# Attention in a perceiver block: scores in three fp32r terms, three keys blocks at the head of a phase, and GpSimd's split in quarters

## The chip, the cores and the metric

The kernel runs on one core of a Trainium2 chip. The metric is the time of one execution on the device in microseconds (us). Engines: TensorE (PE, its weight loads PEld), VectorE (DVE), ScalarE (ACT), GpSimd (POOL), and SyncE (SP), whose queue issues the DMAs. Results of PE go to PSUM, which has eight banks; a bank holds 128 x 512 float32 values.

## The reference

```python
x = x + xattn(layernorm(x), ctx, ctx)   # 16 heads of 32: x (2,128,512), ctx (2,2048,512)
x = x + attn(layernorm(x))              # 16 heads, reshaped without a transposition, layernorm with gamma, beta
x = x + ffn(layernorm(x))               # the expert of 4 that the router's argmax names, gelu, Wo, layernorm
# xattn, for each of 16 heads:
q = Q @ Wq + bq;  k = K @ Wk + bk;  v = V @ Wv + bv
out = softmax(q @ k.T / sqrt(32)) @ v   # then out @ Wo + bo
```

All data are float32. The context (2 x 2048 rows) makes the first attention the largest part of the work.

## The kernel before, in words

The first attention is cut into eight **phases** p = 0 to 7 (NP = 8, G = 4): batch b = p // 4, and in it a group g of four heads (128 of the 512 columns). A phase goes over four blocks c of 512 keys (C = 4, CH = 512). Every engine's program is written out by hand in its order, with waits on semaphores; there is no planner.

**Keys** (`keys`, PE from line 972, DVE line 586). A block's keys, transposed, are the product of the group's columns of Wk with the context, 4 tiles of 128 x 3 terms = 12 products of 512 columns in fp32r: weights and context are each split into a high part in fp32r and the rest (wkH, wkL, ctxH, ctxL), and three of the four cross terms are taken. All products of this form go through the helper `product`, line 969. They land in one bank (K_BANK, 6), and DVE adds the bias and writes `Kr` (line 592). The next keys block waits on PE until DVE has read the bank (`k_done`, line 980).

**Scores** (`scores`, line 1003): four heads, each a float32 product of 32 rows with 512 columns, in banks 0 to 3 (line 1018). DVE's `negative_scores` (line 603) reads each bank, negates, keeps the running minimum and writes `Pm`; the next block's scores of a head wait for that (`s_done`).

**Softmax.** When a phase's four blocks are scored, ACT's `exponentials` (line 367) take a head's 2048 scores at a time. In the *next* phase, PE transposes the probabilities, four 128 x 128 tiles per head and block (`probs_T`, line 1021, operation in line 1032), heads 0 and 2 into bank 4, heads 1 and 3 into bank 5 (T_BANKS). ACT copies heads 0 to 2 to `PT` (line 378), DVE head 3 (line 621). `weighted_values` (line 1036, operation in line 1047) multiplies with V in bank 7.

**The end of a phase.** DVE's `reciprocals` (line 624) inverts the sums and spreads them over 128 columns (`rexp`, line 631); PE's `reciprocals_T` (line 1052) puts them across partitions; ACT copies that to `RT` (line 386); DVE's `outputs` (line 634) multiplies and adds the bias. The first weighted values of a phase wait for the outputs of the phase before (`o_done`).

The main loop of PE (from line 1275) does, in iteration p, the keys and scores of phase p and the transposes and weighted values of phase p - 1:

```python
if more: keys(p, 0)
if late: weighted_values(p - 2, C - 1); reciprocals_T(p - 2)
if more: keys(p, 1)
for c in range(C):
    probs_T(p - 1, c, 0); probs_T(p - 1, c, 1)
    if c == 0 and more: keys(p, 2)
    if c: weighted_values(p - 1, c - 1)
    probs_T(p - 1, c, 2); probs_T(p - 1, c, 3)
    if more:
        scores(p, c)
        if c == 1: keys(p, 3)
```

`late` is true from p = 2 on, except in p = 5. At p = 4 (= G) the loop also does the first batch's second attention and the second batch's 16 value blocks (`while_values`) between each other. Batch 0's later steps are spread over phases 5 to 7 as DVE's `alongside` (line 821): in phase 5 the reciprocals of the second attention's sums (`denominators2`, line 728), its normalised output (`outputs2`) and that output's transposition (`outputs2_T`, line 739, 16 copies); in phase 6 PE's `attention2_out` (line 1175), which writes bank 0 and whose result DVE reads in `added_output2` (line 754) before the scores of phase 6 may write that bank (`u_done`); in phase 7 the router's logits in bank 1, which DVE reads (line 771) before the scores of phase 7 (`logit_done`).

**The context of batch 1** is loaded when phase 3's keys have read batch 0's, and POOL splits it, per block one cast of 128 x 2048 (line 339) and one subtraction (line 341). Phase 4's keys wait for the subtraction (`ctx_split1`).

**SP** loads the second attention's weights one after the other into one tile, `wS` (lines 256 to 262): xWo early, then wq, wk, wv, wo when the last user is done. After the phases come second_experts, first_experts (line 1217) and the output product (line 1271), which the change does not touch.

Of the kernel before, what the change touches and what calls it, by code (L numbers as in the profile page):

```python
# [11 lines left out]
F32 = mybir.dt.float32  # L12
# [5 lines left out]
P = 128  # L18
# [5 lines left out]
def perceiver_block(nc, a, out):  # L24
# [23 lines left out]
    with ExitStack() as ctx:  # L48
# [25 lines left out]
        Kr = at("Kr", [P, C, CH], F32, 176)  # L74
        x = at("x_sb", [P, B, D], F32, 192)
        qT = at("qT", [P, G, TOK], F32, 196)
        attnT = at("attnT", [P, G, TOK], F32, 200)
# [9 lines left out]
        wS = at("wS", [P, KT, D], F32, 184)  # L87
        xbo = at("xbo", [P, D], F32, 184)
# [78 lines left out]
        K_BANK, PV_BANK = 6, 7  # L167
        SPARE = K_BANK
# [35 lines left out]
        k_mm, k_done = sem("k_mm"), sem("k_done")  # L204
# [29 lines left out]
        def _(sp):  # L234
# [21 lines left out]
            sp.wait_ge(x_added, B)  # L256
# [3 lines left out]
            for k, w in enumerate(("wk", "wv", "wo")):  # L260
                sp.wait_ge(qkv_mm[0], k + 1)
                sp.dma_start(wS[:], a[w]).then_inc(wS_in, 16)
            sp.wait_ge(v_mm, B * NV)
            for n in range(3):
# [46 lines left out]
        def _(pool):  # L311
# [24 lines left out]
            for c in range(C):  # L336

                pool.wait_ge(raw_in[c], 32 if c else 16)
                pool.tensor_copy(ctxH[c][:], raw[c][:]).then_inc(ctx_hi1, 1)
                pool.wait_ge(ctx_hi1, c + 1)  # L340
                pool.tensor_tensor(ctxL[c][:], raw[c][:], ctxH[c][:].bitcast(F32), ALU.subtract).then_inc(ctx_split1, 1)
# [6 lines left out]
        def _(act):  # L348
# [32 lines left out]
            def reciprocals_T(p):  # L381

                act.wait_ge(r_mm, p + 1)
                if p:
                    act.wait_ge(o_done, 2 * p)
                act.copy(RT[:], ps[:, PV_BANK, P:2 * P]).then_inc(r_copied, 1)

# [11 lines left out]
            for c in range(1, C):  # L399
                for j in (0, 2):  # L400
                    values(0, c, j)
# [39 lines left out]

            def masks(b):
# [20 lines left out]
            for p in range(1, NP + 1):  # L463
                late = p >= 2 and p != G + 1
                if p != G + 1:
                    exponentials(p - 1, 0)
                    exponentials(p - 1, 1)
                    if late:
                        reciprocals_T(p - 2)
                    exponentials(p - 1, 2)  # L470
                probs_T(p - 1, 0, 0)
# [963 lines left out]
```

## Time and profile before

| | us |
|---|---|
| median of 3 runs | 538.05 |
| their lowest and highest | 537.7, 540.35 |
| the profiled execution's own time | 536.02 |
| its span, from the first to the last instruction | 534.3 |
| busy: PE, PEld, DVE, ACT, POOL | 516.1, 367.6, 294.6, 210.0, 38.3 |
| mean granted clock of TensorE | 0.998 of full speed |

The page has for each engine its busy time and share, the chain of work that ended last, and groups of instructions with the mean duration of one and the idle time ahead of them. Records of PE overlap, because a product's end lies behind the start of the next: the pace is the distance between starts, not the duration. The columns of the trace's other views stand with the rows below.

### The profile page before, as it was taken

Reading aid. Unit: us, or ns where it says so; the run is one execution under the profiler, and the core shown is the slowest. Engines: PE = TensorE matmul, PEld = TensorE weight load, DVE = VectorE, ACT = ScalarE, POOL = GpSimd, SP = SyncE. Lnnn points to the kernel's source line nnn. Section 1 sums busy time; section 2 is a strip of 40 time slices with the busy share of each in tenths; the row PEclk is TensorE's granted clock in tenths of the full one; section 3 lists DMA queues with packets and bytes.
Section 4 is the critical chain, followed back from the end, with each engine's and each line's share of the span. In section 5 each row is a group of like instructions: output and inputs, shape, how many; then the busy total and the mean of one; then the engine's idle time right before and its main releaser. Section 6 shows DMA issues by size and latency. Waiting matters only on the chain.

```text
span 534.3 us, 8854 instructions
## 1 busy us (share of the span) xinstructions
PE 516.1 (97%) x3574; PEld 367.6 (69%) x3574; DVE 294.6 (55%) x606; ACT 210.0 (39%) x305; POOL 38.3 (7%) x32
## 2 busy tenths in 40 slices
PE   8999999999998999999999999988999999999995
PEld 6777776677776777888776678746575445877652
DVE  3645525757576662453496684652275537976332
ACT  4110027273736331455126346373065206745120
POOL 0220000000395000000000000000000010000000
PEclk9999999999999999999999999999999999999999
DMA  8800000000450002330100000590986965874000
GB/s 260 351 0 1 1 0 1 2 1 3 168 216 11 2 2 79 106 132 0 60 2 1 1 2 1 224 404 10 360 340 230 389 253 216 305 284 197 1 20 20
DMA packets 11598, 62.21 MB, mean 116 GB/s; under 512 B 1572, under 2 KB 2596, under 8 KB 4772
## 3 DMA queue, kind: packets, MB, share of 16 engines
q1 hardware_dynamic: 11560, 61.66, 30.7%
q8 instruction: 29, 0.48, 0.4%
q14 instruction: 9, 0.07, 0.0%
HBM read 61.13 MB, written 0.52 MB: 115 GB/s over the span
## 4 chain that ended last, share of the span: by engine, by line
PE 95%; DVE 2%; issue 2%; ACT 1%; POOLq 0%; POOL 0%; DVEq 0%; ACTq 0%
PE ps L969 41%; PE ps L1032 11%; PE ps L1224 10%; PE ps L1018 6%; PE ps L1047 6%; PE ps L1271 5%; PE ps L1251 3%; PE ps L1252 3%; PE ps L1253 3%; PE ps L963 1%; PE ps L1060 1%; PE ps L1234 1%; PE ps L1148 1%; PE ps L1065 1%; PE ps L1069 1%
## 5 line engine op out<-in xcount | busy, mean ns | idle before, releaser
L378 ACT COPY PT<-ps 128x512 f32<-128x512 f32 x96 | 53.3, 588 | 105.1 <-PE ps L1032 105.1
L1032 PEld LDWEIGHTS ps<-ident,Pm 128*128 128x128 f32 x512 | 56.5, 141 | 21.7 <-issue 18.1
L1032 PE MATMUL ps<-ident,Pm 128*128 128x128 f32 x512 | 69.2, 277 | 1.6 <-ACT PT L378 0.7
L612 DVE TENSOR_SCALAR_CACHE_REDUCE Pm<-ps,small 128x512 f32<-128x512 f32 x96 | 66.4, 748 | 7.1 <-PE ps L1018 6.9
L370 ACT ACTIVATE Pm<-Pm,small 128x2048 f32<-128x2048 f32 x32 | 64.2, 2009 | 14.2 <-DVE Pm L612 14.2
L1224 PE MATMUL ps<-w1raw,z 128*128 128x512 f32 x128 | 57.3, 595 | 0.7 <-DVE Pm L612 0.7
L969 PE MATMUL ps<-ctxH,wkH 128*128 128x512 f32 x124 | 51.4, 414 | 2.4 <-DVE Kr L592 2.1
L969 PE MATMUL ps<-wvH,ctxH 128*128 128x512 f32 x124 | 50.0, 403 | 0.0
L969 PE MATMUL ps<-ctxL,wkH 128*128 128x512 f32 x124 | 48.7, 393 | 0.0
L969 PE MATMUL ps<-ctxH,wkL 128*128 128x512 f32 x124 | 48.5, 391 | 0.0
L969 PE MATMUL ps<-wvH,ctxL 128*128 128x512 f32 x124 | 48.4, 390 | 0.0
L969 PE MATMUL ps<-wvL,ctxH 128*128 128x512 f32 x124 | 48.3, 389 | 0.0
L592 DVE TENSOR_SCALAR Kr<-ps,small 128x512 f32<-128x512 f32 x32 | 24.0, 749 | 36.4 <-PE ps L969 34.4
L1224 PEld LDWEIGHTS ps<-w1raw,z 128*128 128x128 f32 x128 | 23.5, 190 | 27.1 <-issue 26.4
L943 DVE TENSOR_TENSOR w2L<-w2raw,w2H 128x2048 fp32r<-128x2048 f32 x16 | 36.2, 2288 | 10.1 <-ACT w2H L547 10.1
L621 DVE COPY PT<-ps 128x512 f32<-128x512 f32 x32 | 22.1, 691 | 30.3 <-PE ps L1032 29.4
L969 PEld LDWEIGHTS ps<-ctxH,wkH 128*128 128x128 f32 x124 | 23.3, 188 | 20.5 <-issue 15.8
L1018 PE MATMUL ps<-Kr,qT 32*128 32x512 f32 x256 | 36.5, 640 | 0.6 <-ACT qT L397 0.6
L547 ACT CAST w2H<-w2raw 128x2048 fp32r<-128x2048 f32 x16 | 30.4, 1910 | 15.1 <-PE ps L1253 15.0
L365 ACT COPY V<-ps 128x512 f32<-128x512 f32 x16 | 9.4, 588 | 66.3 <-PE ps L969 64.4
L1047 PE MATMUL ps<-PT,V 128*32 128x128 f32 x1024 | 34.6, 276 | 0.9 <-DVE PT L621 0.9
L324 POOL TENSOR_TENSOR small<-small 128x1 f32<-128x1 f32 x10 | 6.8, 678 | 372.1 <-DVE small L572 372.1
(162 smaller groups left out, 720.3 us busy)
## 6 DMA issues: line engine op xcount, KB each, us to landing
w1raw<-in_W SPq DMA_DIRECT2D x16, 1024.0 KB, 7.2
w2raw<-in_W SPq DMA_DIRECT2D x16, 1024.0 KB, 4.8
raw<-in_ctxT SPq DMA_DIRECT2D x7, 1024.0 KB, 4.8
woF<-in_ffn_Wo SPq DMA_DIRECT2D x4, 1024.0 KB, 15.9
ctx_first<-in_ctxT SPq DMA_DIRECT2D x4, 256.0 KB, 5.0
wv_raw<-in_xWv SPq DMA_DIRECT2D x2, 512.0 KB, 6.6
wq<-in_xWq SPq DMA_DIRECT2D x1, 1024.0 KB, 11.7
wS<-in_xWo SPq DMA_DIRECT2D x1, 1024.0 KB, 7.0
```

What stands on the lines that cost most here:

```text
L370: act.activation(Pm[:, i, :], Pm[:, i, :], ACT.Exp, bias=mx[:, p % 2, i, C - 1:C], scale=-1.0, accum_out=den[:, p, i:i + 1]).then_inc(exp_ ...
L378: act.copy(PT[:, c % 2, i, :, :].rearrange("p k t -> p (k t)"), ps[:, T_BANKS[i % 2], :]).then_inc(pt_act, 1)
L547: act.copy(w2H[n % 3][:], w2raw[n % RING2][:]).then_inc(w1_hi, 1)
L592: dve.tensor_scalar(Kr[:, c, :], ps[:, K_BANK, :], bias3[:, 1, p % G:p % G + 1], None, ALU.add).then_inc(k_done, 1)
L612: dve.tensor_scalar(Pm[:, i, c * CH:(c + 1) * CH], ps[:, i, :], -1.0, mx[:, p % 2, i, c - 1:c] if c else NOT_YET, ALU.mult, ALU.min, accum ...
L943: dve.tensor_tensor(w2L[n % RING2][:], w2raw[n % RING2][:], w2H[n % 3][:].bitcast(F32), ALU.subtract).then_inc(w1_split, 1)
L969: mm = pe.matmul(dst, l, r, start=(n == 0), stop=(n == len(pairs) - 1))
L1018: pe.matmul(ps[:, i, :], qT[q, g, b * T:(b + 1) * T], Kr[q, c, :], start=True, stop=True)\
L1032: last = pe.transpose(ps[:, T_BANKS[i % 2], j * P:(j + 1) * P], Pm[:, i, c * CH + j * P:c * CH + (j + 1) * P], ident[:])
L1047: last = pe.matmul(ps[q, PV_BANK, 0:T], V[:, c * JT + j, (HPG * g + i) * DH:(HPG * g + i + 1) * DH], PT[:, c % 2, i, j, :], start=(c == 0 ...
L1224: last = pe.matmul(ps[:, c, :], z[:, n, :], w1raw[n % RING][:, c * CH:(c + 1) * CH], start=(n == 0), stop=False)
L1271: last = pe.matmul(ps[:, b, :], hidT[b][:, k, :], woF[:, k, :], start=(k == 0), stop=(k == IT - 1))
```

## The change

Scores are computed in fp32r, in three terms as the keys are: ACT writes the keys with their bias as a high part (`KrH`), DVE the rest (`KrL`), each for three blocks (KR = 3) instead of four; the queries are split likewise at the start (`qH` by ACT, `qL` by DVE). A scores block is 12 products instead of 4. In phases 1 to 7 three keys blocks stand in a row at the head, into banks 6, 3 and 2 (`K_BANKS`), where banks 3 and 2 are those of the scores of heads 3 and 2. The weighted values and reciprocals of p - 2 follow them. The copies of a phase's first transposes (block 0, four heads) are all DVE's, those of blocks 1 to 3 all ACT's. The copy to `RT` moves from ACT to DVE. POOL splits a block in quarters: four casts, four subtractions. `wS` moves to another place and is loaded later, and the second attention's output weight has tiles of its own (`wo2`), loaded once per batch; half of `outputs2_T(0)` goes to ACT; in the part with the value blocks some of these move by one place.

```diff
+        K_BANKS = (K_BANK, 3, 2, K_BANK)
...
-            sp.wait_ge(x_added, B)
+            sp.wait_ge(pv_mm, C * G)
             sp.dma_start(wS[:], a["xWo"]).then_inc(wS_in, 16)
...
+                if n == 7:
+                    sp.wait_ge(qkv_mm[1], 2)
+                    sp.dma_start(wo2[1][:], a["wo"]).then_inc(wo2_in[1], 16)
...
+                for k in range(KT):
+                    pool.tensor_copy(ctxH[c][:, k, :], raw[c][:, k, :]).then_inc(ctx_hi1, 1)
+                for k in range(KT):
+                    pool.wait_ge(ctx_hi1, KT * c + k + 1)
+                    pool.tensor_tensor(ctxL[c][:, k, :], raw[c][:, k, :], ctxH[c][:, k, :].bitcast(F32), ALU.subtract)\
+                        .then_inc(ctx_split1, 1)
...
+            def keys(p, c):
+
+                n = p * C + c
+                bank = K_BANKS[c] if p else K_BANK
+                act.wait_ge(k_mm, n + 1)
+                if n >= KR:
+                    act.wait_ge(s_mm, (n if c == C - 1 else p * C) * HPG - (2 * HPG if c == C - 1 else 0))
+                act.activation(KrH[:, c % KR, :], ps[:, bank, :], ACT.Identity, bias=bias3[:, 1, p % G:p % G + 1],
+                               scale=1.0).then_inc(k_hi, 1)
...
+                act.activation(qH[:, m, :], ps[:, (m + 2) % 4, 0:TOK], ACT.Identity, bias=bqs[:, m:m + 1],
+                               scale=SCALE).then_inc(q_done, 1)
...
+                for c in range(C - 1):
+                    if p != G + 1:
+                        exponentials(p - 1, c)
+                    if p < NP:
+                        keys(p, c)
...
+                dve.wait_ge(k_hi, n + 1)
+                dve.scalar_tensor_tensor(KrL[:, c % KR, :], ps[:, bank, :], bias3[:, 1, p % G:p % G + 1],
+                                         KrH[:, c % KR, :].bitcast(F32), ALU.add, ALU.subtract).then_inc(k_done, 1)
...
+                dve.wait_ge(r_mm, p + 1)
+                dve.tensor_copy(RT[:], ps[:, PV_BANK, P:2 * P]).then_inc(r_copied, 1)
...
-                if p == G + 2 and at_point == "keys1":
+                if p == G + 2 and at_point == "outputs":
                     added_output2(0)
...
                     keys(p, 0)
                     alongside(p, "keys0")
                     keys(p, 1)
+                    alongside(p, "keys1")
+                    keys(p, 2)
+                for i in range(HPG):
+                    probs_T(p - 1, i)
                 if late:
                     outputs(p - 2)
-                alongside(p, "keys1")
-                if p < NP:
-                    keys(p, 2)
+                alongside(p, "outputs")
                 for c in range(C):
-                    probs_T(p - 1, c)
                     if p < NP:
                         negative_scores(p, c)
...
+                if p == G + 1 and c == 2:
+                    pe.wait_ge(rden_ready, 1)
...
+                if p and 0 < c < C - 1:
+                    pe.wait_ge(s_done, p * C * HPG)
...
+                terms = ((qH, KrH), (qL, KrH), (qH, KrL))
+                for k, (l, r) in enumerate(terms):
+                    for i in range(HPG):
+                        q = slice(DH * i, DH * (i + 1))
+                        if n and k == 0:
+                            pe.wait_ge(s_done, (n - 1) * HPG + i + 1)
+                        last = pe.matmul(ps[:, i, :], l[q, g, b * T:(b + 1) * T], r[q, c % KR, :], start=(k == 0),
+                                         stop=(k == len(terms) - 1))
...
                 if more:
                     keys(p, 1)
+                    keys(p, 2)
+                if late:
+                    weighted_values(p - 2, C - 1)
+                    reciprocals_T(p - 2)
...
-                    if c == 0 and more:
-                        keys(p, 2)
```

## Rows read from the trace of the kernel before

**Rows 1.** The page: busy time of each engine, and the chain's shares by line.

```profile
PE 516.1 (97%) x3574; PEld 367.6 (69%) x3574; DVE 294.6 (55%) x606; ACT 210.0 (39%) x305; POOL 38.3 (7%) x32
...
PE ps L969 41%; PE ps L1032 11%; PE ps L1224 10%; PE ps L1018 6%; PE ps L1047 6%; PE ps L1271 5%; PE ps L1251 3%; PE ps L1252 3%; PE ps L1253 3%; PE ps L963 1%; PE ps L1060 1%; PE ps L1234 1%; PE ps L1148 1%; PE ps L1065 1%; PE ps L1069 1%
```

**Rows 2.** Table by stage: phases 2 and 4, length, then each engine's busy time.

```profile
105.71:133.92 28.21, 28.15 (x278) 20.51 (x275) 17.34 (x44) 14.86 (x21) 0.00 (x0) 1.00 0.01 2
162.15:192.82 30.67, 28.46 (x278) 20.58 (x275) 20.25 (x46) 14.98 (x21) 5.70 (x2) 1.00 0.00 1
```

**Rows 3.** Waits of PE: what it waited for, total us, times, longest.

```profile
PE ps L969 <- DVE Kr L592: 2.1, 3, 0.9
PE ps L1055 <- DVE rexp L631: 1.9, 1, 1.9
```

**Rows 4.** Timeline of PE, phase 2's head and phase 3's start: start, duration.

```profile
105.71 0.50 PE L969 MATMUL ps<-ctxH,wkH 128*128 128x512 f32 x1
106.05 0.39 PE L969 MATMUL ps<-ctxH,wkL 128*128 128x512 f32 x1
...
109.92 0.47 PE L969 MATMUL ps<-ctxH,wkH 128*128 128x512 f32 x1
...
116.69 1.03 PE L1032 MATMUL ps<-ident,Pm 128*128 128x128 f32 x8
117.65 1.14 PE L1018 MATMUL ps<-Kr,qT 32*128 32x512 f32 x8
118.73 1.09 PE L1032 MATMUL ps<-ident,Pm 128*128 128x128 f32 x8
...
133.92 0.50 PE L969 MATMUL ps<-ctxH,wkH 128*128 128x512 f32 x1
```

**Rows 5.** Chain in order of time: start, length of the piece, its records.

```profile
46.97 1.07 PE ps L1018 x8
48.04 13.82 PE ps L969 x60
...
395.23 3.44 PE ps L1224 x8
```

**Rows 6.** Timeline of all engines: one scores block, its loads and its products.

```profile
104.64 0.31 PEld L1018 LDWEIGHTS ps<-Kr,qT 32*128 32x128 f32 x8 [0.17 <-issue]
104.64 1.14 PE L1018 MATMUL ps<-Kr,qT 32*128 32x512 f32 x8
```

**Rows 7.** Timelines of POOL and of DVE, head of phase 4.

```profile
163.34 4.59 POOL L341 TENSOR_TENSOR ctxL<-raw,ctxH 128x2048 fp32r<-128x2048 f32 x1
...
165.14 2.87 DVE L631 COPY rexp<-small 128x128 f32<-128x128 f32 x1
```

**Rows 8.** Timeline of DVE: last negative scores of phase 2, first of phase 4.

```profile
136.03 0.75 DVE L612 TENSOR_SCALAR_CACHE_REDUCE Pm<-ps,small 128x512 f32<-128x512 f32 x1
...
177.71 0.69 DVE L612 TENSOR_SCALAR_CACHE_REDUCE Pm<-ps 128x512 f32<-128x512 f32 x1 [0.36 <-PE ps L1018]
...
178.33 0.69 DVE L612 TENSOR_SCALAR_CACHE_REDUCE Pm<-ps 128x512 f32<-128x512 f32 x1
```

**Rows 9.** Timeline, phase 8: a copy on DVE and PE after it.

```profile
359.88 0.69 DVE L621 COPY PT<-ps 128x512 f32<-128x512 f32 x1 [5.05 <-PE ps L1032]
...
360.72 0.63 PE L1032 MATMUL ps<-ident,Pm 128*128 128x128 f32 x4 [0.34 <-DVE PT L621]
```

**Rows 10.** Groups by line: count, busy us, mean ns of one, idle before.

```profile
L378 ACT COPY PT<-ps 128x512 f32<-128x512 f32 x96 | 53.3, 588 | 105.1 <-PE ps L1032 105.1
L621 DVE COPY PT<-ps 128x512 f32<-128x512 f32 x32 | 22.1, 691 | 30.3 <-PE ps L1032 29.4
L731 DVE RECIPROCAL qT<-ps 128x512 f32<-128x512 f32 x1 | 3.3, 3346 | 0.0
L640 DVE TENSOR_TENSOR attnT<-ps,RT 128x128 f32<-128x128 f32 x8 | 2.3, 284 | 5.4 <-ACT RT L386 5.4
L397 ACT ACTIVATE qT<-ps,small 128x256 f32<-128x256 f32 x4 | 1.9, 473 | 5.8 <-PE ps L969 5.8
```

More of the change, by code:

```diff
@@ L379, in probs_T @@
                          ps[:, T_BANKS[i % 2], :]).then_inc(pt_act, 1)
[L381 to L386, printed above, removed]
+            act.wait_ge(bias_in, 16)
+            keys(0, 0)
             for j in (0, 2):
@@ L440, in values2, with outputs2_T @@
                 act.copy(V2[b][:].rearrange("p g d -> p (g d)"), ps[:, 4 * b, :]).then_inc(v2_ready, 1)
+            def outputs2_T(b):
+                act.wait_ge(cN_ready, b + 1)
+                for i in range(2, HPG):
+                    for a in range(HPG):
+                        act.copy(cT[b][DH * a:DH * (a + 1), :, :]
+                                 .rearrange("p m (g i t) -> p m g i t", i=HPG, t=TPH)[:, :, :, i, :],
+                                 cN[b][DH * i:DH * (i + 1), :, :].rearrange("p g (t c) -> p g t c", t=TPH)[:, :, :, a::HPG]
+                                 .rearrange("p g t m -> p m g t")).then_inc(cT_act[b], 1)
             def masks(b):
@@ L668, in _ @@
             values(0, 0, 3)
+            for m in range(G):
+                dve.wait_ge(q_done, 2 * (m + 1))
+                dve.tensor_tensor(qL[:, m, :], qT[:, m, :], qH[:, m, :].bitcast(F32), ALU.subtract).then_inc(q_split, 1)
             negative_scores(0, 0)
@@ L675, in _ @@
                     values(0, c, j)
+                if c == 1:
+                    dve.wait_ge(xbo_in, 16)
+                    dve.wait_ge(norm_done, B)
+                    for b in range(B):
+                        dve.tensor_tensor(x[:, b, :], x[:, b, :], xbo[:], ALU.add).then_inc(x_added, 1)
+                    dve.wait_ge(x_added, B)
                 negative_scores(0, c)
@@ L851, in alongside @@
                     dve.tensor_copy(yT[0][:], split4(ps[:, XT_BANKS[0], :])).then_inc(x2T_done, 1)
-                if p == G + 3 and at_point == "keys1":
+                if p == G + 3 and at_point == "outputs":
                     logits(0)
@@ L983, in keys @@
                 f = slice(g * P, (g + 1) * P)
-                product(ps[:, K_BANK, :], [(w[:, k, f], t[:, k, :]) for k in range(KT)
+                if p and 0 < c < C - 1:
+                    pe.wait_ge(s_done, p * C * HPG)
+                product(ps[:, K_BANKS[c] if p else K_BANK, :], [(w[:, k, f], t[:, k, :]) for k in range(KT)
                                            for w, t in ((wkH, ctxH[c]), (wkL, ctxH[c]), (wkH, ctxL[c]))]).then_inc(k_mm, 1)
@@ L1013, in scores @@
                     pe.wait_ge(logit_done, 1)
-                for i in range(HPG):
-                    q = slice(DH * i, DH * (i + 1))
-                    if n:
-                        pe.wait_ge(s_done, (n - 1) * HPG + i + 1)
-                    pe.matmul(ps[:, i, :], qT[q, g, b * T:(b + 1) * T], Kr[q, c, :], start=True, stop=True)\
-                        .then_inc(s_mm, 1)
+                if p and c == 0:
+                    pe.wait_ge(k_done, n + 3)
+                terms = ((qH, KrH), (qL, KrH), (qH, KrL))
+                for k, (l, r) in enumerate(terms):
+                    for i in range(HPG):
+                        q = slice(DH * i, DH * (i + 1))
[3 more added lines that the diff above has]
+                                         stop=(k == len(terms) - 1))
+                        if k == len(terms) - 1:
+                            last.then_inc(s_mm, 1)
             def probs_T(p, c, i):
@@ L1175, in attention2_out @@
             def attention2_out(b):
-                pe.wait_ge(wS_in, 16 * 5)
-                pe.wait_ge(cT_dve[b], HPG * (2 if b else HPG))
-                if b:
-                    pe.wait_ge(cT_act[b], 2 * HPG)
-                else:
+                pe.wait_ge(wo2_in[b], 16)
+                pe.wait_ge(cT_dve[b], 2 * HPG)
+                pe.wait_ge(cT_act[b], 2 * HPG)
+                if not b:
                     pe.wait_ge(s_done, (G + 2) * C * HPG)
-                product(ps[:, O2_BANKS[b], :], [(cT[b][:, k, :], wS[:, k, :]) for k in range(KT)]).then_inc(o2_mm, 1)
+                product(ps[:, O2_BANKS[b], :], [(cT[b][:, k, :], wo2[b][:, k, :]) for k in range(KT)]).then_inc(o2_mm, 1)
             def normalized_T(b):
```

144 lines of the change are left out of this document (62 added, 82 removed).

## The prediction, made before the change was run

> **What bounds the kernel now.** I read the page's busy line first and then its chain: TensorE (PE) is busy 97% of the 534.3 us span and carries 95% of the chain that ended last, most of it in lines 969 (key and value products) and 1032 (transposes) [rows 1]. So a change pays only if PE's own work shrinks or if PE waits less. The table by stage tells how much waiting there is to win: a steady phase (phase 2) has PE busy 28.15 of 28.21 us, phase 4 only 28.46 of 30.67 [rows 2]. PE's waits agree: 2.1 us in three waits for a keys block to leave its bank and 1.9 us in one wait for the reciprocals' columns [rows 3]. VectorE (DVE) and ScalarE (ACT) have 17.3 and 14.9 us of work in a phase of 28 [rows 2], so neither is a bound by its sum; what counts is the order in which their queues answer PE. The chain in order of time shows phase 2's head as it is: keys, weighted values, reciprocals, keys, transposes, keys, transposes, scores, with PE never free [rows 4]. Each pair of transposes has a keys block behind it, and behind that block the copies are hidden. The change takes this block away.
>
> **Prices of PE's work.** In the chain 60 fp32r products of 512 columns take 13.82 us, 0.23 each, and eight records of float32 products take 3.44, 0.43 each [rows 5]. A product has two such records.
>
> **Scores.** A block of four heads takes 1.07 us now [rows 5]: the heads run side by side, so it is 2 x 0.43 and some 0.21 for the first weight load and the change of shape. Three fp32r terms instead are 3 x 0.23 + 0.21 = 0.90 if the heads stay side by side and the later weight loads stay hidden. Over 32 blocks this is 32 x 0.17 = 5.4 us less. The trace has no fp32r product with 32 rows, so I bound it: at half a float32 record (0.215) the block is 0.86 and the gain 6.7; if each round showed its load (0.11, what the first product after a change of shape lasts longer, 0.50 against 0.39 [rows 4]), it is 3 x 0.34 + 0.10 = 1.12 and this part loses 1.6. I take 0.90, because in the float32 block all eight weight loads are over 0.31 us after its start, under products that run for 1.14 [rows 6].
>
> The Trainium skill speaks against this point (TensorE: Matmul & The Clock Gate, Part 3: Packing small matmuls): a weight load overlaps running products only when its row group is another one. Rounds two and three load the same four row groups again, so by this rule each round would show its load and the sum below would be 7 us higher. The trace does not bear it out, since the second loads of the same row groups lie under the first products there [rows 6].
>
> **Keys in a row.** Phase 2's head, from its first key product to the end of its first scores, takes 118.73 - 105.71 = 13.02 us [rows 4]. In the new order, with no waits: the first keys block with weighted values and reciprocals 4.21 (105.71 to 109.92), two more blocks in a row 2 x 12 x 0.23 = 5.5, the four heads' transposes 2 x 0.96 = 1.9, scores 0.90, in all 12.5. Of the 0.5 saved 0.17 is the scores' and 0.3 is changes of shape that fall away: 7 phases, 2.1 us.
>
> **Waits that go.** Two waits of 0.94 where two keys blocks followed each other in one bank (phases 1 and 5), and phase 4's 1.88 + 0.26 [rows 3]. The latter is POOL's: its subtraction of line 341 runs 4.59 us from 163.34 on, and VectorE's little copy of line 631, begun at 165.14, ends only with it, after 2.87 [rows 7]. Quarters cut such a hold to about 4.59 / 4 = 1.15, and three keys blocks cover the rest. Together 4.0 us. The gains are 5.4 + 2.1 + 4.0 = 11.5.
>
> **Waits that come.** (a) Keys blocks two and three write the banks of scores 2 and 3, so PE waits until VectorE has read all of the last scores. That ends at 136.03 + 0.75, 2.86 after phase 3's first keys product at 133.92 [rows 4, 8]; PE resumes 0.15 after what it waited for (a copy from 359.88 for 0.69, PE at 360.72 [rows 9]). Against 0.11 + 12 x 0.23 = 2.87 for the first block that is 0.15, in six phases 0.9.
>
> (b) The four heads' transposes now run in a row through two banks. The third pair's bank is free when VectorE has copied the first head: 0.69 [rows 10] and 0.2 for the handovers, while PE has one head (0.43: half of a pair's 0.96 [rows 4] less some 0.1 for the change of shape) to do. With the pipelining lost this is 0.6, and the fourth head waits another 0.18, because such passes follow each other at 0.61 or 0.62 (177.71, 178.33 [rows 8]). So 0.8 in phases 2, 3, 4, 6 and 7. In phase 1 no weighted values stand between keys and transposes, and the first copy also stands behind the third block's ScalarE pass (0.59) and VectorE pass (about 0.7) [rows 10]: 1.5. Together 5.5.
>
> (c) VectorE now does a head's outputs, three steps of 0.3 [rows 10], between the last of these copies and the negative scores. From the end of the transposes: last copy 0.2 to 0.8, outputs to 1.7, the four heads' negative scores done at 1.7 + 3 x 0.61 + 0.69 = 4.2, PE back at 4.35. PE has scores, transposes, weighted values and transposes to do, 4.0, and then needs the last head's bank: 0.35 in phases 2 to 4, 1.0. In phase 3 one output step can also meet a POOL quarter (up to 1.15): 0.5.
>
> (d) Phase 5: the third keys block waits for the reciprocal of 3.35 us [rows 10], which starts only after the first block's ScalarE and VectorE passes. From that block's end: 0.2 + 0.6 + 0.7 + 3.35 + 0.15 = 5.0, while PE has one block, 2.8. So 2.2, and then 1.5 as in phase 1: 3.7.
>
> (e) Phase 6: the scores wait for the bank of the second attention's output, which VectorE reads now only after the four copies and the outputs: 1.7 + 0.69 + 0.15, 2.5 us in place of nothing. (f) Phase 7: the router's logits stand in the same place, 1.7 and two short steps: 1.9. (g) At the start the scores wait for a second ScalarE pass over the last queries (0.47 [rows 10]) and a subtraction of half a VectorE pass: 0.8.
>
> **Costed at nothing.** ScalarE's 28 keys passes past phase 0 (0.59 each, 2.4 a phase) go into a queue with 13 us free per phase. The second load of wo is 1 MB in a stretch where SyncE's queue has only weight tiles behind it; the load of xWo now waits for phase 3's last weighted values, but its product also moves back by one value block of 2.8. If that cover were gone, the load would show for a few microseconds, once. Phase 8 has no keys: it loses the wait for a late exponential and gains waits behind VectorE's copies, and I put it at zero, within 1 either way.
>
> **Sum.** 0.9 + 5.5 + 1.5 + 3.7 + 2.5 + 1.9 + 0.8 = 16.8 come, 11.5 go: 5.3 us slower. The profiled execution took 536.0 us (span 534.3), so it would be 541.3; the median of the runs is 538.05, 2.0 above it, and I forecast 543.4 on that scale, 1.0% slower.
>
> **Rivals.** *The head answers in time.* If VectorE copies each head's transposes before PE asks for the bank and reaches the outputs, u and logits while PE is still at keys, (b), (c), (e), (f) and 1.5 of (d) vanish, 12.9 us, and the kernel is 7.6 faster: 530.4. For it: VectorE is idle nearly 11 us per phase. Against it: program order puts all four copies ahead of the outputs, and a copy (0.69) is longer than a head's transposes (0.43). It decides at the gap ahead of the third head: with under 0.1 there, and no gap ahead of phases 6 and 7's first scores, the change is faster.
>
> *Weight loads show.* If rounds two and three of a scores block cannot preload, a block takes 1.12, 0.22 more than forecast: 32 x 0.22 = 7.0, so 550.4. This is the result that the skill's rule would give. Against it stand the loads of the float32 block [rows 6].
>
> *Heads one behind the other.* If fp32r products of different row groups do not run side by side, a block takes 12 x 0.23 + 0.2 = 3.0 and the kernel 32 x 2.1 = 67 us more, about 610. The float32 heads do overlap: eight records of 0.43 are 3.4 one after the other, and the block takes 1.07.
>
> *Gains and waits cancel.* The waits of (b) to (f) are differences of small numbers; if they are 30 to 70% of what I make them, the result lies within 2.7 us of before, 0.5%, which is about what a measurement of this kernel can tell from no change.
>
> **Chances.** Forecast (3 to 9 us slower) 0.48; cancelling 0.22; head in time 0.16; loads show 0.10; heads in series 0.04. So faster 0.16, the same 0.22, slower 0.62. The range runs from the head-in-time case, 530.4, to the loads' case with phase 8's 1 us, 551.4; the serial case lies outside. The forecast's own range is 540.5 to 547.
>
> **What would show it.** PE gaps ahead of the third head's transposes in every phase, released by VectorE's PT copies; one of about 2 us ahead of phase 5's third keys block, released by the reciprocal; about 2 us ahead of the first scores of phases 6 and 7; no gap ahead of line 1055 in phase 4; a scores block near 0.90. If these gaps are there and the time still falls, I mis-sized the scores; if they are absent, my order of VectorE's queue is wrong.

## The result, and the profile after

The changed kernel took 547.76 us (median of 4 runs, 546.74 to 548.56) against 537.88 for the kernel before (4 runs): ratio 1.0192, 95% interval 1.0152 to 1.0233. It is 1.9% slower. The forecast was 543.4: slower, as it came, but 9.9 us were added where 5.3 had been summed. The profiled run took 546.74 us with a span of 544.8, 10.5 more than before's 534.3.

The page, TensorE's busy time, then the chain by engine:

```profile
PE 517.1 (95%) x3702; PEld 375.7 (69%) x3702; DVE 298.3 (55%) x610; ACT 232.4 (43%) x341; POOL 41.5 (8%) x56
...
PE 89%; issue 3%; ACT 3%; DVE 2%; DMA 1%; SPq 1%; POOLq 0%; DVEq 0%
```

PE has lost 2 points of busy share against [rows 1], and of the chain PE's part is 89% where it was 95%. The scores became cheaper and PE is busy 1.0 us longer all the same: some of its work ran slower, which the table by stage explains below. What PE waited for, in place of [rows 3] (us in total, times, longest):

```profile
PE ps L1076 <- DVE PT L643: 4.1, 5, 1.4
PE ps L1060 <- issue: 4.0, 2, 2.3
PE ps L1002 <- issue: 2.2, 1, 2.2
...
PE ps L1060 <- DVE qL L695: 1.4, 1, 1.4
PE ps L1076 <- ACT Pm L394: 1.3, 3, 0.4
PE ps L1090 <- DVE attnT L666: 0.9, 2, 0.7
PE ps L1248 <- DVE KrL L614: 0.8, 1, 0.8
```

Line 1076 is the transposes, 1060 the scores, 1002 keys and values, 1090 the weighted values, 1248 the masks. Both old waits, for Kr and for rexp, are gone; these seven are new or longer. Two of the names need care. "issue" says that the profile names no releaser: the 2.2 of line 1002 ends with VectorE's reciprocal in phase 5 (261.66 to 265.01, PE back at 265.11), and the 4.0 of line 1060 is taken apart by e1 and e2 below. And the three waits put down to ScalarE's Pm are the gap of 0.44 ahead of the third head in phases 2 to 4: that head's exponential was done at 114.23 in phase 2, and e3 takes the gap away. PE's timeline of phase 2:

```profile
115.51 1.04 PE L1076 MATMUL ps<-ident,Pm 128*128 128x128 f32 x8
116.98 1.22 PE L1076 MATMUL ps<-ident,Pm 128*128 128x128 f32 x8 [0.44 <-ACT Pm L394]
118.14 0.51 PE L1060 MATMUL ps<-KrH,qH 32*128 32x512 f32 x4
118.47 0.40 PE L1060 MATMUL ps<-KrH,qL 32*128 32x512 f32 x4
118.71 0.40 PE L1060 MATMUL ps<-KrL,qH 32*128 32x512 f32 x4
119.04 1.10 PE L1076 MATMUL ps<-ident,Pm 128*128 128x128 f32 x8
```

The scores block takes 0.90 from start to start (118.14 to 119.04). The table by stage, phases 2, 4, 5 (from its second keys block on), 6, 7 and one stretch of phase 6 (length, busy time of PE, PEld, DVE, ACT, POOL, then the granted clock, as in [rows 2]):

```profile
105.53:133.88 28.35, 27.91 (x295) 21.41 (x291) 17.43 (x45) 17.13 (x24) 0.00 (x0) 1.00 0.01 1
163.15:191.53 28.38, 27.93 (x295) 21.41 (x291) 21.88 (x47) 17.13 (x24) 7.45 (x9) 1.00 0.01 2
260.10:287.17 27.07, 23.46 (x245) 17.79 (x243) 20.54 (x44) 12.36 (x24) 0.00 (x0) 1.00 0.08 25
287.17:323.88 36.71, 33.98 (x302) 24.67 (x298) 21.97 (x55) 17.23 (x24) 1.10 (x2) 0.91 0.01 2
323.88:357.06 33.18, 30.20 (x315) 23.46 (x311) 19.52 (x53) 17.72 (x25) 0.00 (x0) 1.00 0.26 101
304.80:311.60 6.80, 6.01 (x55) 4.53 (x56) 5.66 (x15) 1.17 (x2) 0.55 (x1) 0.50 0.01 2
```

Phase 2 is as long as in [rows 2] (28.35 against 28.21), phase 4 2.3 shorter, phase 7 2.8 longer (33.18 against 30.38), and phase 6 5.3 longer than in the kernel before, whose row of the same table is

```profile
286.04:317.41 31.37, 31.37 (x287) 22.01 (x283) 21.60 (x54) 14.86 (x21) 1.10 (x2) 1.00 0.01 1
```

PE's busy time in phase 6 grew by 2.6: from 304.8 to 311.6 the granted clock was 0.50, the lower of the two levels (1.2 GHz, not 2.4). PE's timeline there:

```profile
302.08 1.22 PE L1076 MATMUL ps<-ident,Pm 128*128 128x128 f32 x8 [0.44 <-DVE PT L643]
305.59 0.80 PE L1060 MATMUL ps<-KrH,qH 32*128 32x512 f32 x4 [2.28 <-issue]
306.15 0.66 PE L1060 MATMUL ps<-KrH,qL 32*128 32x512 f32 x4
306.57 0.66 PE L1060 MATMUL ps<-KrL,qH 32*128 32x512 f32 x4
307.17 1.97 PE L1076 MATMUL ps<-ident,Pm 128*128 128x128 f32 x8
309.07 1.94 PE L1090 MATMUL ps<-PT,V 128*32 128x128 f32 x32
```

The forecast's wait (e) stands at 305.59, 2.28 us long. Behind it the scores take 1.58 from start to start, the transposes 1.90 and the weighted values 1.86, where phase 2's take 0.90, 1.02 and 1.02. The stretch costs 2.7 us that no step of mine had. A second stretch at 0.50, from 513.0 to 516.4, just behind the short products of expert_bias, costs some 1.6 more; the profiled run of before had none there. In the 60 us ahead of it PE has no pause over 0.12 us, and of the runs below e8, e10 and e11 have no such stretch while the others do, so it belongs to the single execution and not to the change.

### The profile page after: what moved, and what is told of

It is laid out like the page before. It is cut to its first block, busy times and chain, and to the rows that moved or that the text cites. A ratio compares the mean times of both kernels' runs of the same rounds, so it can differ in the third digit from the quotient of the medians.

```text
span 544.8 us, 9149 instructions
## 1 busy us (share of the span) xinstructions
PE 517.1 (95%) x3702; PEld 375.7 (69%) x3702; DVE 298.3 (55%) x610; ACT 232.4 (43%) x341; POOL 41.5 (8%) x56
## 4 chain that ended last, share of the span: by engine, by line
PE 89%; issue 3%; ACT 3%; DVE 2%; DMA 1%; SPq 1%; POOLq 0%; DVEq 0%
PE ps L1002 39%; PE ps L1076 10%; PE ps L1265 10%; PE ps L1090 6%; PE ps L1060 5%; PE ps L1312 5%; PE ps L1292 3%; PE ps L1293 3%; PE ps L1294 3%; PE ps L996 1%; DMA wv_raw<-in_xWv 1%; ACT KrH L380 1%; PE ps L1275 1%; PE ps L1190 1%; ACT Pm L394 1%
## 5 line engine op out<-in xcount | busy, mean ns | idle before, releaser
L402 ACT COPY PT<-ps 128x512 f32<-128x512 f32 x96 | 51.7, 589 | 64.9 <-PE ps L1076 64.9
L1076 PE MATMUL ps<-ident,Pm 128*128 128x128 f32 x512 | 71.4, 281 | 6.1 <-DVE PT L643 4.1
L614 DVE SCALAR_TENSOR_TENSOR KrL<-ps,small,KrH 128x512 fp32r<-128x512 f32 x32 | 23.8, 747 | 40.7 <-ACT KrH L380 40.7
L380 ACT ACTIVATE KrH<-ps,small 128x512 fp32r<-128x512 f32 x32 | 22.0, 688 | 51.0 <-PE ps L1002 50.3
L1090 PEld LDWEIGHTS ps<-PT,V 128*32 128x32 f32 x1024 | 26.6, 112 | 9.1 <-issue 7.5
L623 DVE COPY V<-ps 128x512 f32<-128x512 f32 x16 | 11.0, 690 | 35.6 <-PE ps L1002 35.5
```

The lines of the kernel that those rows point to most:

```text
L380: act.activation(KrH[:, c % KR, :], ps[:, bank, :], ACT.Identity, bias=bias3[:, 1, p % G:p % G + 1], scale=1.0).then_inc(k_hi, 1)
L402: act.copy(PT[:, c % 2, i, :, :].rearrange("p k t -> p (k t)"), ps[:, T_BANKS[i % 2], :]).then_inc(pt_act, 1)
L1076: last = pe.transpose(ps[:, T_BANKS[i % 2], j * P:(j + 1) * P], Pm[:, i, c * CH + j * P:c * CH + (j + 1) * P], ident[:])
L1090: last = pe.matmul(ps[q, PV_BANK, 0:T], V[:, c * JT + j, (HPG * g + i) * DH:(HPG * g + i + 1) * DH], PT[:, c % 2, i, j, :], start=(c == 0 ...
```

## The experiments

The edits are shown shortened, some lines of them in words; e1 to e3, e6 to e8 and e12 are one execution each.

**Does the order of VectorE's queue make the phase heads late?** My theory: steps (b) to (f) are all VectorE's order at the head of a phase. The first two runs take the second attention's sum (e), and then the logits too (f), ahead of the four copies on VectorE.

```
             if late:
                 outputs(p - 2)
+            alongside(p, "copies")     # e1: added_output2(0); e2: logits(0) too
             for i in range(HPG): probs_T(p - 1, i)
```

> The changed kernel with one thing moved: in phase 6 VectorE reads the second attention's output (added_output2) ahead of the four copies of transposes instead of behind them and the outputs. My theory (VectorE's order makes the wait, and the wait lets PE's clock fall): the gap of 2.28 us ahead of phase 6's first scores goes under 0.3, the stretch of half clock that began in it (6.8 us, worth 3.0) does not come, and the span falls by some 5 us from 544.8. Rival (the clock's fall has another cause, such as the new scores): the gap goes, the stretch of half clock stays in phase 6, and the span falls by 2.3 only.

> As the run before, and in phase 7 VectorE also reads the router's logits ahead of the copies. My theory: the gap of 1.75 us ahead of phase 7's first scores goes under 0.3, and the 0.78 ahead of the masks in phase 7, which VectorE's late third key pass makes, shrinks too: 1.7 to 2.5 us below the run with added_output2 alone, 7 to 7.5 below 544.8. Rival (PE waits there for the copies or the keys in any case): the gaps stay above 1 us in sum and the span differs by under 1 us from the run with added_output2 alone.

545.51 and 543.24 us. In e1 the 2.28 ahead of phase 6's scores is gone, and the third head's transposes wait 0.73 instead of 0.44; phase 6 is 33.14 instead of 36.71, and no half clock comes at 305. But a stretch at 0.50 now comes in phase 5, at 266.0, between the two pauses there (2.16 and 1.45), so the whole won only 1.2. In e2 phase 7's 1.75 goes as well (31.56 instead of 33.19 in e1). The span came out 2.3 below e1 but 3.5 below the changed kernel where I had expected 7 to 7.5, and the 0.78 ahead of the masks, expected to shrink, stayed. So (e) and (f) were order, as forecast; the half clock moves between pauses of about 2 us (in e2 it stands at 266.4).

**Is it the bank or the copies?** The third head's transposes get a third PSUM bank, so they no longer wait for VectorE's first copy.

```
-  bank = T_BANKS[i % 2]
+  bank = (4, 5, K_BANK, 4)[i] if c == 0 and p < B * G - 1 else T_BANKS[i % 2]
```

> The changed kernel with a third bank for the first transposes: head 2's go to the keys' bank 6, head 3's to bank 4, so that head 2 need not wait for VectorE's copy of head 0. Theory A (two banks are the price, step b of the prediction): the gap of 0.44 ahead of the third head goes in phases 2, 3, 4, 6 and 7 and about 0.7 us a phase with it, 3 to 4 us in all. Theory B (VectorE's queue is: four copies, outputs, negative scores one behind the other): the gap goes, but the copies end only 0.2 us earlier, so the second scores block waits longer for its last bank (0.16 to 0.3 us now, 0.7 to 1.0 then), and the span falls by 1 to 1.5 us only.

544.73 us. The 0.44 goes from phases 2, 3, 4, 6 and 7, but 0.21 to 0.26 come back behind the first scores, and the pauses ahead of the scores grow by 0.29: 2.57 in phase 6 and 2.04 in phase 7, for 2.28 and 1.75. Phase 2 is 0.26 shorter (28.09), as theory B had it: a bank hands most of the wait on, and VectorE's four copies in a row are late. The span fell by 2.0, between the two theories; 1.1 of it is in phase 3 (28.17 for 29.27), where the output step did not meet POOL.

**Undo the third block in a row.** Two keys blocks stay in a row; the third goes back between the two pairs of transposes, the weighted values and reciprocals behind the first keys block, and VectorE does outputs, u and logits ahead of the copies. ScalarE's and VectorE's passes over the keys move with the blocks.

```
-  K_BANKS = (K_BANK, 3, 2, K_BANK)
+  K_BANKS = (K_BANK, 3, K_BANK, K_BANK)
   probs_T(p - 1, c, 0); probs_T(p - 1, c, 1)     # PE
+  if c == 0 and more: keys(p, 2)
   probs_T(p - 1, c, 2); probs_T(p - 1, c, 3)
```

> The changed kernel without the row of three: keys block 2 stands between the two pairs of transposes again and in bank 6, weighted values and reciprocals behind the first keys block, VectorE's outputs, added_output2 and logits ahead of the four copies, its third key pass behind the first negative scores; fp32r scores, quarters on GpSimd, two key banks and the copies' split stay. My theory (the row of three and the order it forces cost all of the loss, the rest is a gain): no gap above 0.6 us in phases 1 to 7, scores blocks of 0.90, no stretch of half clock there, and a span near 526: 5.4 less for the scores, 1.9 for two gaps, 2.1 for GpSimd's hold, 0.4 for small gaps, 0.8 to 1.6 more at the start and in phase 5; so about 1.5% faster than before. Rival (the fp32r scores cost elsewhere what they save, through ScalarE's and VectorE's extra key passes): a span of 532 to 536, no faster than before.

537.54 us (10 runs, 534.27 to 539.02) against 539.1: ratio 0.9973, interval 0.9942 to 1.0003. Every pause of (b) to (f) is gone but for 0.48 in phase 5 and less than 0.2 in phases 1 and 3: phase 2 takes 27.39, 0.82 less than before, phase 6 30.70. That is 10 us off the changed kernel: the order of the keys blocks and of VectorE's queue, moved together here, had cost them. Yet the span near 526 of my theory was missed (536.3), and in time the rival's "no faster than before" came, though not for its reason: one new wait stands in phase 4, where the reciprocals' product is again needed early:

```profile
162.18 1.08 PE L1085 MATMUL ps<-PT,V 128*32 128x128 f32 x32
168.32 0.79 PE L1093 MATMUL ps<-ident,rexp 128*128 128x128 f32 x2 [5.06 <-DVE rexp L651]
168.76 0.77 PE L999 MATMUL ps<-ctxH,wkH 128*128 128x512 f32 x1
```

A pause of 5.06 us, and key products at half speed behind it (granted clock 0.50 from 166.4 to 173.2): phase 4 took 34.60. VectorE's and POOL's timelines there:

```profile
162.24 6.02 DVE L651 COPY rexp<-small 128x128 f32<-128x128 f32 x1
...
160.99 2.29 POOL L351 CAST ctxH<-raw 128x512 fp32r<-128x512 f32 x4
163.25 4.93 POOL L354 TENSOR_TENSOR ctxL<-raw,ctxH 128x512 fp32r<-128x512 f32 x4
```

In [rows 7] the copy was held 2.87 us by one whole instruction. Here it is held through POOL's quarters, six ends of which fall inside it, and ends 0.08 after the last (163.25 + 4.93 = 168.18). My "quarters cut such a hold to about 4.59 / 4" is wrong for this copy. The changed kernel shows the same, harmless because three keys blocks cover it: its copy runs 4.53 us from 166.16, to the end of the quarters that POOL began at 165.56 (5.05).

**What ends the hold?** Three runs on e4: POOL whole again (e6), each quarter's cast followed by its own subtraction (e12), and no copy at all (e5: PE reads the reciprocals' columns as repeated stationary operands).

```
 # e6
-  for k in range(KT): cast quarter k
-  for k in range(KT): subtract quarter k
+  cast block; subtract block
 # e12
-  for k in range(KT): cast quarter k
-  for k in range(KT): subtract quarter k
+  for k in range(KT): cast quarter k; subtract quarter k
 # e5
-  dve.tensor_copy(rexp[:], recip...to_broadcast([P, HPG, DH]))
-  pe.matmul(ps[:, PV_BANK, P:2 * P], rexp..., ident[:])
+  for i in range(HPG):
+      pe.matmul(ps[DH * i:DH * (i + 1), PV_BANK, P:2 * P], recip[:, i:i + 1].to_broadcast([P, DH]), ident[:])
```

> The kernel e4_keys2_between with POOL's split again in two whole instructions a block, as in the kernel before. The prediction's reading: a hold of VectorE's little copy ends with the POOL instruction that runs, so quarters shorten it; then the whole instructions give a hold as long or longer than e4's 6.02 us, and a time of 537 to 541. Rival: the copy gets its turn only where POOL pauses; quarters issued back to back leave no pause, and whole instructions leave one of about 0.08 us between cast and subtraction (163.26 to 163.34 in the trace of before). Then the copy, begun near 162.2 in the cast, ends near 163.6, a hold of 1.1 to 1.5 us, the gap ahead of the reciprocals' product falls to under 0.8 us, and the time falls by 4 to 8 us to 530 to 534.

533.57 us: the time that the rival named (530 to 534), but not its mechanism, for the hold was longer than 1.5 us and the gap than 0.8. The copy began only after POOL's subtraction had (162.32 and 161.20), so the pause between cast and subtraction was not met; it was held to the instruction's end, 3.52 us, and PE's gap was 2.56. Whole instructions are also quicker, 6.5 us a block for 7.2, so POOL was done earlier. Against the first reading, whole was better than quarters.

> The kernel e4_keys2_between with POOL's quarters in another order: cast and subtraction of one quarter, then of the next, where e4 has four casts and then four subtractions. Now every subtraction waits for the cast just ahead of it, so POOL pauses (some 0.08 us, as between 163.26 and 163.34 in the trace of before) four times a block; in e4 the quarters follow each other without a pause. In e4 VectorE's copy began at 162.24, under a cast, and ended at 168.26 with POOL's last quarter at 168.18, past the ends of six or seven quarters. Theory: VectorE gets its turn at a pause, not at the end of an instruction. Then the copy in phase 4 ends at the next pause, 0.3 to 2 us after it began, the gap ahead of the reciprocals' product is under 1 us, phase 4 takes 27.4 to 28.5 us instead of 34.6 and the time is 529 to 533. Rival: a copy once held stays held until POOL has nothing left to do; then it takes 5 to 6 us again, with a gap of 4 to 5 us, and the time is 535 to 539.

529.99 us. VectorE's and POOL's timelines of e12:

```profile
162.61 0.62 DVE L650 COPY rexp<-small 128x128 f32<-128x128 f32 x1
...
161.86 1.28 POOL L353 TENSOR_TENSOR ctxL<-raw,ctxH 128x512 fp32r<-128x512 f32 x1
163.09 0.61 POOL L351 CAST ctxH<-raw 128x512 fp32r<-128x512 f32 x1
163.78 1.30 POOL L353 TENSOR_TENSOR ctxL<-raw,ctxH 128x512 fp32r<-128x512 f32 x1
```

The copy took 0.62 and ended 0.09 after the subtraction under which it began; phase 4 takes 27.46 and the clock stays at 1.0. The rival falls, since POOL still had a whole block to do. The theory is not shown by it: that subtraction is the last of its block, so the copy met no end of a quarter inside a block. The boundary it came through is that between two blocks, where the next cast follows without a measurable pause but with a wait for its block's load of its own. In e4, e6 and the changed kernel the copy ended with the last instruction that POOL had. Whether the order of the quarters decides stays open.

Not every VectorE instruction is held like this copy. In phase 3 the last step of a head's outputs (line 642 before, 661 in e9) begins under a cast of POOL's first block. VectorE's and POOL's timelines of the kernel before, then of e9, a later version with quarters in e4's order:

```profile
142.16 1.75 DVE L642 TENSOR_SCALAR attnT<-attnT,small 128x128 f32<-128x128 f32 x1
141.93 1.90 POOL L339 CAST ctxH<-raw 128x2048 fp32r<-128x2048 f32 x1 [112.02 <-DMA raw<-in_ctxT]
...
141.34 0.54 DVE L661 TENSOR_SCALAR attnT<-attnT,small 128x128 f32<-128x128 f32 x1
141.19 2.29 POOL L351 CAST ctxH<-raw 128x512 fp32r<-128x512 f32 x4 [109.61 <-DMA raw<-in_ctxT]
```

Before, the step was held to the end of the whole cast, 1.75 us for a usual 0.29. In e9 it was let in after the first of four quarters that follow one another without a pause, and ended at 141.88; in e4, e5 and e10 the same step took 0.62, 0.65 and 0.63 and ended 0.07 to 0.08 after the quarter under which it began. So quarters did cut the hold of this step, and did not cut that of the column copy. What tells the two apart is open.

> The kernel e4_keys2_between, but the reciprocals are no longer spread to 128 columns by VectorE: TensorE reads each head's column as a repeated stationary operand, in four products of 32 columns. In e4 the only large gap left is 5.06 us at 163.26, while VectorE's copy (begun at 162.24, 6.02 us long) ends with POOL's last quarter at 168.18, and a stretch at half the granted clock from 166.4 to 173.2 follows. Theory: the copy is the only thing held and the clock falls because of that pause. Then the gap ahead of the reciprocals' product in phase 4 is under 0.4 us, the granted clock stays 1.0 from 160 to 175, phase 4 is 7 to 8 us shorter than in e4 and the span of the profiled run is near 529 (time 530.5). Rival 1: POOL's splitting itself or ScalarE's passes are late, so the gap only moves to the next keys block or the scores of phase 4: phase 4 is under 2 us shorter and the time is within 1.5 us of e4's 537.5. Rival 2: the gap goes but the half clock comes anyway: some 5 us shorter than e4.

528.81 us (4 runs) against 535.93: ratio 0.9842, interval 0.9799 to 0.9884. Phase 4 takes 27.39 with PE busy throughout, and the half clock at 166 is gone. The copy was all that PE had waited for there; both rivals fall.

**Does a pause alone make the clock fall?** The kernel before, float32 scores and all, with a pause put in by hand.

```
 # VectorE, phase 6
+  for _ in range(4): the first copy of the probabilities once more
   dve.tensor_copy(PT..., ps[:, T_BANKS[1], :])
+  added_output2(0)     # moved here, from ahead of the copies
```

> The kernel before, with one pause put in by hand: in phase 6 VectorE repeats its first copy of the probabilities four times and only then adds the second attention's output, on which the scores of phase 6 wait. Both theories: a TensorE gap of 4 to 5 us ahead of the first scores of phase 6, near 303. Theory: such a pause is enough for the granted clock to fall, so a stretch at half of it begins in the pause or right behind it, 3 to 7 us long, and the span grows by the pause and 1.5 to 3.5 us more, 6 to 8.5 in all. Rival: the new scores' products with 32 rows are what lets the clock fall in the changed kernel; then the float32 kernel keeps a granted clock of 1.0 through phase 6 and its span grows by 4 to 5.2 us only.

546.3 us, span 544.7. Phase 6, the stretch of half clock in it, and PE's timeline:

```profile
286.21:324.60 38.39, 34.06 (x286) 23.51 (x282) 24.45 (x58) 14.96 (x21) 1.10 (x2) 0.91 0.00 1
304.50:311.30 6.80, 5.59 (x48) 3.50 (x48) 5.61 (x15) 1.17 (x2) 0.55 (x1) 0.50 0.01 2
```

```profile
300.34 1.04 PE L1037 MATMUL ps<-ident,Pm 128*128 128x128 f32 x8
305.71 2.09 PE L1023 MATMUL ps<-Kr,qT 32*128 32x512 f32 x8 [4.33 <-issue]
307.73 1.97 PE L1037 MATMUL ps<-ident,Pm 128*128 128x128 f32 x8
```

Phase 6 grew by 7.0: 4.33 of pause and 2.7 of slow products, with not one fp32r score in it. The theory holds for a pause of this length, the rival falls. (The span grew by 10.4, more than the 6 to 8.5 expected: the rest is two more stretches at 0.50 in the tail, 458.1 and 512.7, as other runs have there.)

**What makes the scores block 0.90?** The changed kernel with the loops exchanged: three terms of one head, then the next head.

```
-  for k, (l, r) in enumerate(terms):
-      for i in range(HPG):
+  for i in range(HPG):
+      for k, (l, r) in enumerate(terms):
```

> The changed kernel with the two loops of its scores exchanged: the three terms of one head one after the other, then the next head, instead of one term of all four heads. Same products. Theory: the block's 0.90 us comes from four heads of different row groups side by side, round by round; head by head the three products of one head follow each other at 0.23 or more and only the seams between heads overlap, so a block takes 1.9 to 2.8 us and the kernel is 30 to 60 us slower. Rival: the order does not matter, a block stays at 0.9 to 1.0 and the time within 3 us of the changed kernel's 547.8.

546.14 us: my theory falls and the rival holds. PE's timeline of e8, one block:

```profile
118.45 0.52 PE L1060 MATMUL ps<-KrH,qH 32*128 32x512 f32 x4
118.78 0.42 PE L1060 MATMUL ps<-KrH,qL 32*128 32x512 f32 x4
119.02 0.42 PE L1060 MATMUL ps<-KrL,qH 32*128 32x512 f32 x4
119.37 1.09 PE L1076 MATMUL ps<-ident,Pm 128*128 128x128 f32 x8
```

The block takes 0.92, round by round as if the program had said so: the four heads' first products start together at 118.45, ahead of the first head's second one (118.78), which stands before three of them in the program.

**What are the fp32r scores worth in a good order?** e5 with float32 scores and unsplit keys.

```
-  terms = ((qH, KrH), (qL, KrH), (qH, KrL))
+  terms = ((qT, KrL),)     # KrL holds the whole float32 keys; no ScalarE pass, no q split
```

> The kernel e5_no_column_copy with the scores in float32 again: one product of four heads from the unsplit queries and keys, no second ScalarE pass for them. Order, banks and everything else stay as in e5. Theory: the three fp32r terms are what the forecast made them, 0.17 us a block less than float32, so each block takes 1.07 instead of 0.90 and the kernel is 31 x 0.17 = 5.3 us longer than e5, 534; the start gives 0.8 back, so 533 to 534.5. Rival: the extra passes for the split (ScalarE and VectorE one after the other ahead of the scores) cost what the shorter products gain, so the time is within 2 us of e5's 528.8.

532.69 us (4 runs), ratio to before 0.9877 (0.9841 to 0.9912), where e5 had 0.9842: about 2 us longer than e5 by these ratios, the rival's figure, not 5.3. The two intervals overlap, and the times as they stand are 3.9 apart, so the traces have to decide: the first experts' product behind phase 7 starts at 343.68 in e10 and at 341.49 in e5, 2.2 later. Phase 2 of e10:

```profile
104.82:132.70 27.88, 27.88 (x284) 20.48 (x280) 17.12 (x44) 14.50 (x20) 0.00 (x0) 1.00 0.01 2
```

Its blocks take 1.07, so the 0.17 is right; but the phase is longer by 0.49, not 4 x 0.17 = 0.68, and pauses that e5 has (0.48 in phase 5, 0.78 ahead of the masks, 0.2 in phase 1) are absent in e10. The split's second pass makes the keys later: in phase 2 VectorE's pass over the keys starts 0.5 after the third keys block does in e5 (112.63, 112.15) and 0.6 ahead of it in e10 (112.06, 112.66), and the copies stand behind that pass.

**A version that beats both.** e9 is e5 with two waits moved; e11 is e9 with POOL whole.

```
-  if p == G + 3 and c == 2: masks(0)
   if c: weighted_values(p - 1, c - 1)
+  if p == G + 3 and c == 2: masks(0)
-  pe.wait_ge(q_split, G)
+  pe.wait_ge(q_done, 2 * G)      # and q_split, g + 1 ahead of each phase's first scores
```

> The kernel e5_no_column_copy with two small waits moved: in phase 7 the router's masks stand behind the weighted values of that place instead of ahead of them (e5 waits 0.78 us there at 331.74), and the first scores wait for the last ScalarE pass over the queries but only for the first column block's subtraction (1.39 us at 31.26 in e5). Theory: both waits are cover that is missing, so the first falls under 0.1 and the second to 0.9 to 1.1, and the time is 0.9 to 1.3 us below e5's 528.8, near 527.7. Rival: the masks now hold up the third head's transposes behind them by as much (their copy by ScalarE comes before that head's copy), and the first scores still wait for the queries' last pass: within 0.4 us of e5.

529.57 us (6 runs), ratio 0.9806 (0.978 to 0.9832). The masks' wait is gone and the start's is 0.93, so phase 7 takes 29.42 instead of 30.39. In phase 4, however, one output step was held by POOL's quarters (1.22 instead of 0.29) and PE waited 0.78.

> The kernel e9_best with POOL's split in two whole instructions a block again. In e6 a block took POOL 6.5 us whole, in e4 7.2 in quarters, and with the columns' copy gone nothing in phase 4 waits for POOL. Theory: quarters are worth nothing in this order; time within 0.6 us of e9_best. Rival: the keys of phase 4 or VectorE's output steps in phases 3 and 4 still meet POOL, and the longer instruction holds them longer: 1 to 3 us slower than e9_best with a gap in phase 3 or 4 that e9_best does not have.

527.9 us (4 runs) against 539.78: ratio 0.9777, interval 0.9748 to 0.9806, the best of all, 2.2% under the kernel before. The wait of phase 4 is gone (28.34 in e9, 27.38 here); that is neither expectation, for quarters cost instead of being worth nothing. Phases 2 and 4 of e11:

```profile
104.33:131.72 27.39, 27.39 (x301) 21.11 (x297) 17.11 (x44) 17.02 (x24) 0.00 (x0) 1.00 0.01 1
159.12:186.50 27.38, 27.38 (x300) 21.11 (x296) 17.20 (x45) 17.02 (x24) 6.57 (x3) 1.00 0.01 2
```

## Why the prediction was right in sign and short in size

Step by step, the trace after against the sum (differences of PE's gaps and of blocks from start to start):

| Step | forecast | measured |
|---|---|---|
| scores, 0.17 a block | -5.4 | -5.4 (block 0.90) |
| keys in a row | -2.1 | 0 |
| waits that go | -4.0 | -4.0 (0.94, 0.94, 1.88 + 0.26) |
| (a) keys wait for negative scores | +0.9 | 0 |
| (b) third and fourth head | +5.5 | +4.7 (5 x 0.63, 1.56 in phase 1) |
| (c) second scores block, phase 3's output step | +1.5 | +1.3 |
| (d) phase 5 | +3.7 | +3.8 (2.16 and 1.63) |
| (e) phase 6 | +2.5 | +2.3 |
| (f) phase 7 | +1.9 | +1.75 |
| (g) start | +0.8 | +0.8 |
| sum | +5.3 | +5.25 |
| half clock, phase 6 | not seen | +2.7 |
| half clock, tail (of this execution) | not seen | +1.6 |
| masks wait for the last keys' pass | not seen | +0.7 |
| phase 8 | 0 | -0.6 |

That is 9.7 of the span's 10.5; the remaining 0.8 I did not follow.

Right: the waits (b) to (g), each within 0.8 of its size and at the place named; e1 to e4 show for (b) to (f) that they are the order of the keys blocks and of VectorE's queue. The scores' price was right too: the rounds start 0.33 and 0.24 apart, and the block takes 0.90. By the Trainium skill's rule on weight loads (TensorE: Matmul & The Clock Gate, Part 3: Packing small matmuls) loads of a row group in use would have shown, 1.12 by the prediction's estimate; the trace disagrees.

Wrong, and by how much: "keys in a row" was sized at 0.3 a phase from a head of 12.5; three blocks in a row take 8.64 (105.53 to 114.17), not 2.95 + 5.5 = 8.45, and the transposes without their pause 2.0, not 1.9: nothing was saved. That error of 2.1 was hidden, by luck, by (a) and (b), which came out 1.7 smaller.

The step that failed is the one that is not there: the sum charged each new wait at its length, as if PE went on behind it at full speed. Behind phase 6's pause of 2.28 it went on at half the clock, and that cost 2.7; e7 shows that a pause of 4.33 us alone is enough for it, and e1 that phase 6's stretch goes with its pause. The masks' wait, 0.7, was missing too: I did not list it among what stands behind VectorE's new queue. That is 3.4 of the 5 us between the sum and the span; the 1.6 in the tail is this execution's. The median, 547.76, lies above the forecast's own range (540.5 to 547) and inside the whole one only because its upper end had been set for weight loads that show, which did not come: that much was luck.

"Quarters cut such a hold" was wrong for the column copy as well (4.53 in the changed kernel); here only the other half of that sentence, three keys blocks of cover, saved phase 4. The kernel lost because the third keys block, where it stood between the transposes, had been the cover for VectorE's copies: with it back there and the held copy removed, the kernel is 1.6 to 2.2% faster than before (e5, e11), and float32 scores reach 1.2% of that (e10).

Of the rivals, the head in time falls by the gaps of 0.44 and 2.28, and both scores rivals, loads shown and heads in series, by the block of 0.90. Cancelling falls too: the waits came to 14.7 of the 16.8 forecast.

## What to carry to other kernels

Price a new wait at its length, and then ask what TensorE's granted clock does behind it: a pause of 4.3 us cost 7.0 here. When a block of TensorE work is moved, first list what it covered where it stood: its own time changes by nothing, the work that it hid becomes the wait. And splitting a long instruction into pieces need not let the other engine in between them: here it did so for one instruction (0.54) and not for another (6.02). Look at the held instruction's own row, not at the length of a piece.

## What was not expected of the hardware

- Half clock after pauses. Pauses of 4.33 (e7) and 5.06 us (e4) brought 6.8 us at a granted clock of 0.50 each. At pauses near 2 us it came in some runs and not in others: in the changed kernel behind phase 6's 2.28 but not behind phase 5's 2.16; in e1 at phase 5's, in e6 behind 2.56; not in the kernel before behind 1.88. In e8 it came behind phase 7's 1.75 as well, and the stretch in the tail came with no such pause ahead of it. What decides between them is open.
- A held VectorE copy can stay held across the ends of POOL instructions that follow one another: 6.02 us in e4, past five ends to the sixth. Another instruction is let in at the next end: the output step of 0.54 in e9. The Trainium skill (SBUF — State Buffer, Who interferes with whom) says of GpSimd and of VectorE in its two-port modes that whichever issues first has the shared ports for its whole instruction. e6's 3.52 and e9's 0.54, both to the end of one instruction, agree; e4's 6.02 goes beyond it.
- Products of different row groups overtake each other: in e8 all four heads' first products start within 0.03 us (118.45 to 118.48), although the program has two more products of a head ahead of the next head's first. The Trainium skill (TensorE: Matmul & The Clock Gate, Part 3: Packing small matmuls) says that products start strictly in program order; this trace does not bear that out.
